# Four units' rows in flight and a later down product in a routed FFN's expert loop (one core, fp32 split in three)

## Chip, cores and metric

One core of one Trainium2 chip. The metric is the device time of one execution in microseconds, the median of the runs. The kernel before takes 964.21 us.

## What is computed

A linear attention with elu feature maps and a mixture of experts, both on the same input of 16 batches x 512 tokens x 256, summed with the input. The part around the change is the mixture: each of the 8192 tokens goes through 4 of 16 experts, each an up product, silu, and a down product weighted by the router.

```python
combine = zeros((T, E)).at[arange(T)[:, None], topk_idx].add(topk_w)   # T = 8192, E = 16, TOP_K = 4
up = jnp.einsum('th,ehi->eti', x, expert_up)                            # 256 -> 128
down = jnp.einsum('eti,eih->eth', jax.nn.silu(up), expert_down)         # 128 -> 256
moe_out = jnp.einsum('te,eth->th', combine, down)
shared = jax.nn.silu(x @ shared_up) @ shared_down
x = x + attention(layernorm(x)) + (moe_out + shared)
```

## The kernel before

All five engines run programs written out in full, with semaphores between them. Until about 490 us the 16 batches go through attention, shared FFN and router, and GpSimd scatters each token's row (its inputs, weights and running sum) into a region of its experts in HBM. A plan then splits the regions into 143 **units** of 256 rows of one expert: 128 that the tokens could fill, and 15 for the experts' remainders. From then on every engine goes through the units in order:

- **SP** loads a unit's rows (`load_rows`, 272 KB, its `dma_start` is line 453) and, later, its running sums (`load_sums`, line 465). Rows of unit u wait for `fu_done`, the count of up products: from unit 16 on for up(u-6). In each step the sums of the unit 3 before follow; they wait for `added`, the landings of the scatters of the 8th unit before and of those on which its tokens depend. Rows and sums have 8 buffers each.
- **PE** in step u: up product of u (helper `split3`, line 326; 6 matmuls, since each fp32 product is made from high and low parts: high by high, high by low, low by high), transposing of the rows of u+2 (`turn_rows`, line 1572, 4 transposes into a bank `A[u % 2]`), and the down product of u-1 (`unit_down`, 6 matmuls, into `A[2]`, `A[3]` or the two halves of `bank_y` in turn).
- **ACT** in step u: silu of u (line 800), the high part of the transposed rows of u+2 (`rows_high`, line 762), the high part of the silu values of u (line 805), a copy of the expert's up weights for u+2 (`stage`, line 774, into 4 buffers). The last 15 units' rows are loaded by ACT, under a condition.
- **VectorE** in step u: the rows' weights (line 1320) and the low part of the transposed rows of u+2 (`rows_low`, line 1323), the low part of the silu values of u (`hidden_rest`, line 1365), then for u-1 (`sum_up`) the ids of where each row goes on (line 1336, needs the sums loaded) and the weighted sum (line 1341, two instructions, needs the down product).
- **GpSimd** scatters the sums of u back to HBM, in two indirect DMAs (line 628). They wait for VectorE's sum, for the landing of the scatter of u-4, and from unit 10 on the first also for the down product of u+1, the second for the up product of u+3.

Semaphores: `fx_done`, `fx_hi`, `fx_lo` rows transposed, high, low; `fu_done` up product; `fs_done` silu; `fh_hi`, `fh_lo` silu values high, low; `fd_done` down product; `y_ready` summed. The trace names the tiles by their memory: rows `xn` or `x_in`, transposed rows high and low `xt_h`, `xt_l`, silu `hid`, its parts `hs_h`, `hs_l`, weights `k_h` or `k_l_p`, up product `bank_x`, down product `bank_a` or `bank_y` from `we`.

## Time and profile before

| | |
|---|---|
| median of 3 runs | 964.21 us (960.75 to 968.95) |
| profiled execution | 958.44 us, of it the span of the profile 956.7 us |
| experts' loop | about 490 to 925 us of the span, 143 units |
| busy share over the span | PE 80%, VectorE 74%, GpSimd 61%, ACT 58% |
| DMA | 194.66 MB, mean 203 GB/s over the span |
| granted TensorE clock, mean over the span | 0.945 of full |

The profile is one execution taken by the hardware profiler, times in us from the span's start. A line of the profile is a line of the kernel file. PE's matmuls are pipelined and their ends are modelled, so a busy PE isn't PE at its peak. The releaser of a wait is inferred from semaphore events; "issue" means that nothing the profile shows was waited for, "remote" that the releaser is not told.

### The profile page before, as it was taken

The page shows a single profiled execution, that of the slowest core. Times are in us where ns is not written, and L with a number is a line of the kernel's source. Part 1 is how long each engine was busy: PE and PEld are TensorE (multiplying, and loading weights), DVE is VectorE, ACT ScalarE, POOL GpSimd, SP SyncE. Part 2 cuts the span into 40 slices and gives each one's busy share as a digit, 9 for nine tenths or more (in the row PEclk, how much of TensorE's full clock was granted, in tenths as well). Part 3 has the DMA queues.
Part 4 walks back from the last instruction along what each step waited for, and adds up shares of the span by engine and source line. Part 5 has one row for each costly group of instructions (what it writes and reads, how often), then busy time and mean ns, then how long its engine had stood idle before and what let it go on. Part 6 is the DMA issues. An engine that isn't in the chain of part 4 may idle for free.

```text
span 956.7 us, 19946 instructions
## 1 busy us (share of the span) xinstructions
PE 762.2 (80%) x5232; PEld 696.8 (73%) x5232; DVE 703.3 (74%) x2409; ACT 559.5 (58%) x1174; POOL 579.6 (61%) x581
## 2 busy tenths in 40 slices
PE   4999999999999999997377776766777767767762
PEld 4899898999889988886266666765666767656751
DVE  6989988888888999988366766656666566666653
ACT  5778777777677766663155655445555455545541
POOL 1077766666777766667455556665666566565554
PEclk9999999999999999999699999899899799899897
DMA  5245545554445433333398888888788878889790
GB/s 157 89 161 191 187 176 187 190 187 180 145 160 193 147 124 125 119 114 124 121 330 256 267 259 263 259 260 257 240 265 256 256 241 267 263 247 283 232 341 19
DMA packets 137551, 194.66 MB, mean 203 GB/s; under 512 B 16593, under 2 KB 112993, under 8 KB 137441
## 3 DMA queue, kind: packets, MB, share of 16 engines
q1 hardware_dynamic: 107200, 109.23, 38.9%
q0 software_dynamic: 28064, 81.93, 22.2%
q10 hardware_dynamic: 2176, 2.23, 0.8%
q8 instruction: 45, 0.74, 0.4%
q14 instruction: 66, 0.53, 0.2%
HBM read 104.19 MB, written 105.04 MB: 219 GB/s over the span
## 4 chain that ended last, share of the span: by engine, by line
PE 62%; DVE 14%; issue 12%; another core or an unknown queue 5%; ACT 3%; DMA 2%; DVEq 1%; POOL 0%; SPq 0%; ACTq 0%; POOLq 0%
PE bank_a L326 27%; PE bank_x L326 14%; PE bank_y L326 14%; PE bank_a L1572 5%; DVE hs_l L1365 2%; DVE xn L1110 2%; DVE xn L1341 2%; DVE xt_l L1323 1%; PE bank_a L1412 1%; ACT xt_h L762 1%; DVE w L1320 1%; DMA xn<-in_L_attn_bo_dram 1%; DMA k_f<-rows_by_expert 1%; DVE k_f L1341 1%
## 5 line engine op out<-in xcount | busy, mean ns | idle before, releaser
L539 POOL DMA_INDIRECT rows_by_expert<-xn,slots_now x192 | 195.4, 1018 | 120.3 <-PE bank_a L326 63.0
L628 POOL DMA_INDIRECT rows_by_expert<-xn,f_id x128 | 125.5, 981 | 84.9 <-issue 28.1
L1323 DVE TENSOR_TENSOR xt_l<-bank_a,xt_h 128x512 fp32r<-128x512 f32 x143 | 98.2, 687 | 90.9 <-ACT xt_h L762 69.1
L326 PE MATMUL bank_a<-we,hs_h 128*128 x288 | 67.6, 328 | 94.3 <-DVE hs_l L1365 58.1
L800 ACT ACTIVATE hid<-bank_x 128x256 f32<-128x256 f32 x143 | 55.1, 385 | 142.6 <-PE bank_x L326 74.7
L762 ACT CAST xt_h<-bank_a 128x512 fp32r<-128x512 f32 x143 | 83.8, 586 | 80.7 <-PE bank_a L1572 47.5
L326 PEld LDWEIGHTS bank_a<-we,hs_h 128*128 128x128 f32 x288 | 49.0, 206 | 108.8 <-issue 108.8
L545 POOL DMA_INDIRECT rows_by_expert<-xn,slots_now x64 | 80.0, 1250 | 29.8 <-issue 13.2
L326 PE MATMUL bank_y<-we,hs_h 128*128 x284 | 68.6, 334 | 36.9 <-DVE hs_l L1365 20.5
L326 PE MATMUL bank_y<-ws,hs_h 128*128 128x256 f32 x512 | 95.4, 284 | 0.5 <-DVE hs_l L1078 0.5
L326 PE MATMUL bank_x<-xt_h,ws 128*128 128x512 f32 x256 | 92.1, 401 | 0.1
L326 PEld LDWEIGHTS bank_y<-we,hs_h 128*128 128x128 f32 x284 | 50.3, 210 | 50.4 <-issue 49.8
L326 PEld LDWEIGHTS bank_y<-ws,hs_h 128*128 128x128 f32 x512 | 81.8, 190 | 4.2 <-DVE hs_l L1078 0.7
L326 PE MATMUL bank_y<-ws,hs_l 128*128 128x256 f32 x256 | 72.7, 284 | 0.0
L326 PE MATMUL bank_x<-xt_h,k_h 128*128 128x256 f32 x288 | 70.2, 305 | 0.8 <-DVE xt_l L1323 0.8
L326 PE MATMUL bank_x<-xt_h,k_l_p 128*128 128x256 f32 x284 | 66.6, 296 | 1.4 <-DVE xt_l L1323 1.4
L710 ACT ACTIVATE k_f<-bank_a,minus_one 128x256 f32<-128x256 f32 x64 | 30.3, 474 | 57.7 <-issue 41.2
L1365 DVE TENSOR_TENSOR hs_l<-hid,hs_h 128x256 fp32r<-128x256 f32 x143 | 59.9, 419 | 3.5 <-issue 1.8
L805 ACT CAST hs_h<-hid 128x256 fp32r<-128x256 f32 x143 | 59.5, 416 | 0.1
L675 ACT ACTIVATE hid<-bank_x 128x512 f32<-128x512 f32 x64 | 37.7, 589 | 34.1 <-remote 24.4
L326 PEld LDWEIGHTS bank_x<-xt_h,k_h 128*128 128x128 f32 x288 | 55.8, 214 | 1.1 <-DVE xt_l L1323 1.0
L326 PEld LDWEIGHTS bank_x<-xt_h,ws 128*128 128x128 f32 x256 | 48.2, 188 | 9.2 <-DVE ws L922 0.3
(314 smaller groups left out, 2601.2 us busy)
## 6 DMA issues: line engine op xcount, KB each, us to landing
xn<-rows_by_expert SPq DMA_DIRECT2D x132, 272.0 KB
x_in<-rows_by_expert SPq DMA_DIRECT2D x80, 272.0 KB
rows_by_expert<-spare SPq DMA_DIRECT2D x22, 544.0 KB
x_in<-in_L_attn_x_dram SPq DMA_DIRECT2D x16, 512.0 KB
out_dram<-rows_by_expert SPq DMA_DIRECT2D x16, 512.0 KB
k_f<-rows_by_expert SPq DMA_DIRECT2D x16, 272.0 KB
q_f<-rows_by_expert SPq DMA_DIRECT2D x16, 272.0 KB
spare<-rows_by_expert SPq DMA_DIRECT2D x16, 272.0 KB
```

Source lines behind the costliest of these rows:

```text
L326: last = nc.tensor.matmul(dst, a, b, start=start and k == 0, stop=stop and k == n - 1, skip_group_check=mixed)
L539: G.indirect_dma_start(out=half_rows[:, :], in_=xn[:, c % NB, s, 0:RW], in_offset=None, out_offset=bass.IndirectOffsetOnAxis(ap=slots_now[ ...
L545: G.indirect_dma_start(out=by_expert[:, :], in_=xn[:, c % NB, s, :], in_offset=None, out_offset=bass.IndirectOffsetOnAxis(ap=slots_now[:, ...
L628: G.indirect_dma_start(out=half_rows[:, :], in_=f_y[u % YB][:, tile], in_offset=None, out_offset=offset).then_inc(added[u % CLS], 16)
L675: S_.activation(hid[:, n % 2], X[n % 2][:, :], ACT.Silu).then_inc(silu_done, 1)
L710: S_.activation(k_f[:, s, :], A[s][:, 0:D], ACT.Exp, bias=minus_one[:, 0:1])
L762: S_.copy(f_h[u % 4], A[u % 2][:, :].rearrange("p (c s t) -> p c s t", c=KD, s=2)).then_inc(fx_hi, 1)
L800: S_.activation(f_hid[u % 2], X[u % 2][:, 0:UR], ACT.Silu).then_inc(fs_done, 1)
L805: S_.copy(f_hh[u % 2], f_hid[u % 2]).then_inc(fh_hi, 1)
L1323: V.tensor_tensor(f_l[u % 4], A[u % 2][:, :].rearrange("p (c s t) -> p c s t", c=KD, s=2), f_h[u % 4].bitcast(F32), ALU.subtract).then_inc ...
L1365: V.tensor_tensor(f_hl[u % 2], f_hid[u % 2], f_hh[u % 2].bitcast(F32), ALU.subtract).then_inc(fh_lo, 1)
L1572: last = T_.transpose(A[u % 2][:, (2 * h + tile) * P:(2 * h + tile + 1) * P], f_rows[u % RB][:, tile, h * P:(h + 1) * P], ident[:, :])
```

## The change

From unit 14 (`FROM`) on, PE, ACT and VectorE treat the rows of u+3 in step u (transpose, high part, low part), and the down product and the weighted sum are those of u-2. In step 14 itself the rows of two units are treated (16 and 17) and there is no down product. For this the transposed rows rotate over four banks `A[0..3]`, the down product of a unit lies in one bank of `bank_y` (both tiles side by side, units in turn), the high and low parts of the silu values have 3 buffers, the rows' weights 8. The gates follow: GpSimd's second scatter of u waits for the up product of u+4 from unit 14 on; SP's rows of u wait for up(u-7) rather than up(u-6) from unit 16 on; the sums are loaded 5 steps behind the rows rather than 3 from there; ACT's loads of the last rows go out one step earlier. The copy of the up weights (`stage`) stays 2 ahead. The core of the diff:

```diff
@@ -265,14 +265,17 @@
         c_ends_i, c_ends_n = [reused(over_beats, (1, B), i * B, 1)[:, 0].bitcast(U32) for i in range(2)]
         c_before = reused(over_beats, (1, B), 2 * B, 1)[:, 0]
         c_class_i, c_class_n, c_need = [reused(over_beats, (CLS, B), (3 + i * CLS) * B, 1).bitcast(U32) for i in range(3)]
-        w2 = sb("w2", [P, 4, 2])
+        WB = 8
+        AB = 4
+        FROM = 14
+        w2 = reused(over_beats, (WB, 2), E * E - WB * 2)
         f_h = [reused(xt_h, (KD, 2, P), i * KD * UR) for i in range(4)]
         f_l = [reused(xt_l, (KD, 2, P), i * KD * UR) for i in range(4)]
         f_w = [reused(t, (2, UPW), i * 2 * UPW) for t in (k_h, k_l_p) for i in range(2)]
         f_hid = [reused(hid, (1, UR), i * UR)[:, 0] for i in range(2)]
-        f_hh = [reused(hs_h, (1, UR), i * UR)[:, 0] for i in range(2)]
-        f_hl = [reused(hs_l, (1, UR), i * UR)[:, 0] for i in range(2)]
-        f_dn = [[A[2], A[3]], [Y[:, 0, :], Y[:, 1, :]]]
+        f_hh = [reused(hs_h, (1, UR), i * UR)[:, 0] for i in range(3)]
+        f_hl = [reused(hs_l, (1, UR), i * UR)[:, 0] for i in range(3)]
+        f_dn = [[Y[:, i, t * D:(t + 1) * D] for t in range(2)] for i in range(2)]
 
         wk_loaded, wq_loaded, wo_loaded, wv_loaded, bias_loaded = sems(
             "wk_loaded", "wq_loaded", "wo_loaded", "wv_loaded", "bias_loaded")
@@ -364,6 +367,17 @@
             else:
                 eng.wait_ge(raw_loaded, 64 * (i - SH + 3 if i else 1))
 
+        def turned_with(u):
+            if u in (0, FROM):
+                return {0: (), FROM: (u + 2, u + 3)}[u]
+            v = u + (2 if u < FROM else 3)
+            return (v,) if 1 < u and v < UNITS else ()
+
+        def down_with(u):
+            if u < 3 or u == FROM:
+                return ()
+            return (u - 1 if u < FROM else u - 2,)
+
         def unit_rows(first_row, half):
             return by_expert[bass.ds(first_row, UR), half * RW:(half + 1) * RW].rearrange("(s p) r -> p s r", p=P)
 
@@ -440,7 +454,7 @@
             row_of = {}
 
             def load_rows(u):
-                wait(sp, fu_done, u - RB + (3 if u >= 2 * RB else 1))
+                wait(sp, fu_done, u - RB + (2 if u >= 2 * RB else 1))
                 if u == 4:
                     sp.wait_ge(attn_ready, SUB * B)
                 row = row_of[u] = four_from(mybir.EngineType.SP, 0, u, 0, SLOTS - UR)
@@ -468,7 +482,7 @@
 
             ROWS_AHEAD = 7
             SUMS_AHEAD = 4
-            for u in range(SUMS_BY_ACT + ROWS_AHEAD - SUMS_AHEAD):
+            for u in range(SUMS_BY_ACT + ROWS_AHEAD - SUMS_AHEAD + 2):
                 if LAST_SET_LOADED <= u < LAST_SET_LOADED + SET_PARTS:
                     load_set_part(SH + E - 1, u - LAST_SET_LOADED)
                 if u == EARLY - 1:
@@ -479,6 +493,8 @@
                 elif u < SUMS_BY_ACT:
                     row_of[u] = four_from(mybir.EngineType.SP, 0, u, 0, SLOTS - UR)
                 v = u - (ROWS_AHEAD - SUMS_AHEAD)
+                if u >= 2 * RB:
+                    v = u - 5 if u >= 2 * RB + 2 else -1
                 if 0 <= v < EARLY // 2 or EARLY - 1 <= v < SUMS_BY_ACT:
                     load_sums(v)
 
@@ -622,7 +638,7 @@
                         if tile == 0:
                             pool.wait_ge(fd_done, min(u + 2, UNITS))
                         else:
-                            pool.wait_ge(fu_done, min(u + 4, UNITS))
+                            pool.wait_ge(fu_done, min(u + (4 if u < FROM else 5), UNITS))
                     offset = bass.IndirectOffsetOnAxis(ap=f_id[:, u % YB, tile:tile + 1], axis=0)
                     if u < SKIPPED:
                         G.indirect_dma_start(out=half_rows[:, :], in_=f_y[u % YB][:, tile], in_offset=None,
@@ -759,7 +775,7 @@
             def rows_high(u):
                 act.wait_ge(fx_done, u + 1)
                 wait(act, fu_done, u - 3)
-                S_.copy(f_h[u % 4], A[u % 2][:, :].rearrange("p (c s t) -> p c s t", c=KD, s=2)).then_inc(fx_hi, 1)
+                S_.copy(f_h[u % 4], A[u % AB][:, :].rearrange("p (c s t) -> p c s t", c=KD, s=2)).then_inc(fx_hi, 1)
 
             act.wait_ge(plan_ready, 1)
 
@@ -798,11 +814,11 @@
                 act.wait_ge(fu_done, u + 1)
                 wait(act, fh_lo, u - 1)
                 S_.activation(f_hid[u % 2], X[u % 2][:, 0:UR], ACT.Silu).then_inc(fs_done, 1)
-                if 1 < u and u + 2 < UNITS:
-                    rows_high(u + 2)
+                for v in turned_with(u):
+                    rows_high(v)
                 act.wait_ge(fs_done, u + 1)
-                wait(act, fd_done, u - 1)
-                S_.copy(f_hh[u % 2], f_hid[u % 2]).then_inc(fh_hi, 1)
+                wait(act, fd_done, u - 2)
+                S_.copy(f_hh[u % 3], f_hid[u % 2]).then_inc(fh_hi, 1)
                 if u == 1:
                     rows_high(2)
                     stage(2)
@@ -812,8 +828,8 @@
                     stage(u + 2)
                 if u in (4, 18):
                     set_high(SH + E - 2 + (u == 18))
-                if SKIPPED <= u + 6 < UNITS:
-                    load_last_rows(u + 6)
+                if SKIPPED <= u + 7 < UNITS:
+                    load_last_rows(u + 7)
                 if u >= SUMS_BY_ACT:
                     load_last_sums(u)
 
@@ -1316,11 +1332,11 @@
             def rows_low(u):
                 expert = expert_from(experts, u)
                 dve.wait_ge(rows_loaded[u % RB], 16 * (u // RB + 1))
-                wait(dve, y_ready, u - 3)
-                V.tensor_copy(w2[:, u % 4, :], f_rows[u % RB][:, :, bass.ds(expert + D, 1)]
+                wait(dve, y_ready, u - WB + 1)
+                V.tensor_copy(w2[:, u % WB, :], f_rows[u % RB][:, :, bass.ds(expert + D, 1)]
                               .rearrange("p s o -> p (s o)")).then_inc(w2_ready, 1)
                 dve.wait_ge(fx_hi, u + 1)
-                V.tensor_tensor(f_l[u % 4], A[u % 2][:, :].rearrange("p (c s t) -> p c s t", c=KD, s=2),
+                V.tensor_tensor(f_l[u % 4], A[u % AB][:, :].rearrange("p (c s t) -> p c s t", c=KD, s=2),
                                 f_h[u % 4].bitcast(F32), ALU.subtract).then_inc(fx_lo, 1)
 
             def sum_up(u):
@@ -1338,7 +1354,7 @@
                 dve.wait_ge(w2_ready, u + 1)
                 for tile in range(2):
                     y = f_y[u % YB][:, tile, 0:D]
-                    last = V.scalar_tensor_tensor(out=y, in0=f_dn[u % 2][tile][:, 0:D], scalar=w2[:, u % 4, tile:tile + 1],
+                    last = V.scalar_tensor_tensor(out=y, in0=f_dn[u % 2][tile], scalar=w2[:, u % WB, tile:tile + 1],
                                                   in1=y, op0=ALU.mult, op1=ALU.add)
                 last.then_inc(y_ready, 1)
 
@@ -1362,12 +1378,12 @@
 
             def hidden_rest(u):
                 dve.wait_ge(fh_hi, u + 1)
-                V.tensor_tensor(f_hl[u % 2], f_hid[u % 2], f_hh[u % 2].bitcast(F32), ALU.subtract
+                V.tensor_tensor(f_hl[u % 3], f_hid[u % 2], f_hh[u % 3].bitcast(F32), ALU.subtract
                                 ).then_inc(fh_lo, 1)
 
             rows_low(0)
             rows_low(1)
-            for u in range(UNITS + 1):
+            for u in range(UNITS + 2):
                 if u == 2:
                     sum_up(1)
                     hidden_rest(2)
@@ -1375,8 +1391,8 @@
                     hidden_rest(3)
                     sum_up(2)
                 next_experts(experts, mybir.EngineType.DVE, u)
-                if 1 < u and u + 2 < UNITS:
-                    rows_low(u + 2)
+                for v in turned_with(u):
+                    rows_low(v)
                 if u < UNITS and u not in (2, 3):
                     hidden_rest(u)
                 if u == 1:
@@ -1384,7 +1400,8 @@
                     rows_low(2)
                     rows_low(3)
                 if u >= 4:
-                    sum_up(u - 1)
+                    for v in down_with(u):
+                        sum_up(v)
                 if u in (3, 16):
                     set_shape(SH + E - 2 + (u == 16))
                 if u in (6, 20):
@@ -1566,10 +1583,10 @@
 
             def turn_rows(u):
                 pe.wait_ge(rows_loaded[u % RB], 16 * (u // RB + 1))
-                wait(pe, fx_lo, u - 1)
+                wait(pe, fx_lo, u - AB + 1)
                 for h in range(KD):
                     for tile in range(2):
-                        last = T_.transpose(A[u % 2][:, (2 * h + tile) * P:(2 * h + tile + 1) * P],
+                        last = T_.transpose(A[u % AB][:, (2 * h + tile) * P:(2 * h + tile + 1) * P],
                                             f_rows[u % RB][:, tile, h * P:(h + 1) * P], ident[:, :])
                 last.then_inc(fx_done, 1)
 
@@ -1583,15 +1600,15 @@
                 moving = [we[:, bass.ds(expert, 1), i, UPW:].rearrange("p o d -> p (o d)") for i in range(2)]
                 pe.wait_ge(fh_lo, v + 1)
                 wait(pe, y_ready, v - 1)
-                if v == 1:
+                if v == 0:
                     pe.wait_ge(y_summed, B)
                 for tile in range(2):
                     cols = slice(tile * P, (tile + 1) * P)
-                    last = split3(f_dn[v % 2][tile][:, 0:D],
-                                  [(f_hh[v % 2][:, cols], f_hl[v % 2][:, cols], moving[0], moving[1])])
+                    last = split3(f_dn[v % 2][tile],
+                                  [(f_hh[v % 3][:, cols], f_hl[v % 3][:, cols], moving[0], moving[1])])
                 last.then_inc(fd_done, 1)
 
-            for u in range(UNITS + 1):
+            for u in range(UNITS + 2):
                 next_experts(experts, mybir.EngineType.PE, u)
                 if u < UNITS:
                     pe.wait_ge(fx_lo, u + 1)
@@ -1601,15 +1618,15 @@
                            [(f_w[u % 4][:, 0, h * I:(h + 1) * I], f_w[u % 4][:, 1, h * I:(h + 1) * I],
                              f_h[u % 4][:, h].rearrange("p s t -> p (s t)"),
                              f_l[u % 4][:, h].rearrange("p s t -> p (s t)")) for h in range(KD)]).then_inc(fu_done, 1)
-                if 1 < u and u + 2 < UNITS:
-                    turn_rows(u + 2)
+                for v in turned_with(u):
+                    turn_rows(v)
                 if u == 1:
                     unit_down(0)
                     turn_rows(2)
                     unit_down(1)
                     turn_rows(3)
-                if u >= 3:
-                    unit_down(u - 1)
+                for v in down_with(u):
+                    unit_down(v)
 
 
 # ---- launch: one core; inputs and outputs as the reference has them ----
```

## Rows read from the trace of the kernel before

**Rows 1.** Stretches: us, busy us (instructions), clock, DMA share; DMA of 560 to 900.

```profile
core 0: us, PE busy (x) PEld busy (x) DVE busy (x) ACT busy (x) POOL busy (x), PEclk, DMA share, GB/s
490.00:500.00 10.00, 6.72 (x45) 6.28 (x45) 5.61 (x17) 5.10 (x12) 4.72 (x5) 0.83 1.00 331
560.00:600.00 40.00, 30.58 (x213) 27.85 (x213) 26.87 (x88) 22.22 (x52) 24.50 (x26) 0.93 0.85 267
600.00:650.00 50.00, 35.11 (x242) 32.32 (x241) 29.83 (x89) 25.41 (x60) 30.02 (x31) 0.91 0.85 259
650.00:700.00 50.00, 33.55 (x235) 30.41 (x234) 29.69 (x89) 25.44 (x60) 28.94 (x31) 0.93 0.83 249
700.00:750.00 50.00, 37.47 (x264) 34.17 (x263) 32.15 (x97) 25.88 (x62) 30.91 (x33) 0.93 0.81 252
...
925.00:957.00 32.00, 10.10 (x75) 8.79 (x73) 13.44 (x41) 7.95 (x19) 16.13 (x17) 0.79 0.30 89
...
DMA packets 66442, 87.41 MB, mean 257 GB/s; under 512 B 6668, under 2 KB 59690, under 8 KB 66396
```

**Rows 2.** Groups, 560 to 900 us: busy us, mean ns | idle before, releasers.

```profile
L628 POOL DMA_INDIRECT rows_by_expert<-xn,f_id x104 | 101.7, 978 | 68.5 <-issue 23.5 <-PE bank_y L326 14.5 <-remote 8.8
L1323 DVE TENSOR_TENSOR xt_l<-bank_a,xt_h 128x512 fp32r<-128x512 f32 x104 | 71.5, 687 | 72.4 <-ACT xt_h L762 54.5 <-issue 17.8
...
L1365 DVE TENSOR_TENSOR hs_l<-hid,hs_h 128x256 fp32r<-128x256 f32 x104 | 43.5, 418 | 0.0
...
L1572 PE MATMUL bank_a<-ident,xn 128*128 128x128 f32 x208 | 34.4, 292 | 0.0
...
L774 ACT CAST k_h<-we 128x512 fp32r x52 | 32.7, 629 | 0.0
...
L1336 DVE TENSOR_TENSOR f_id<-xn,nowhere 128x2 uint32<-128x2 uint32 x51 | 8.0, 157 | 0.0
```

**Rows 3.** Who waited for whom, 560 to 900 us: total, times, longest.

```profile
ACT hid L800 <- PE bank_x L326: 57.4, 38, 4.6
DVE xt_l L1323 <- ACT xt_h L762: 54.5, 22, 4.0
...
PE bank_a L326 <- DVE hs_l L1365: 46.7, 20, 4.2
ACT xt_h L762 <- PE bank_a L1572: 28.6, 20, 3.9
...
ACT xt_h L762 <- remote: 25.2, 12, 3.9
```

**Rows 4.** Timeline of smooth units: start, us, instruction, [idle before].

```profile
704.96 0.17 DVE L1320 COPY w<-xn 128x2 f32 x1 [0.29 <-DVE k_f L1341]
...
707.11 0.41 ACT L805 CAST hs_h<-hid 128x256 fp32r<-128x256 f32 x1
...
707.28 0.17 DVE L1320 COPY w<-xn 128x2 f32 x1 [0.37 <-issue]
...
707.41 0.62 ACT L774 CAST k_h<-we 128x512 fp32r x1
...
707.96 0.42 DVE L1365 TENSOR_TENSOR hs_l<-hid,hs_h 128x256 fp32r<-128x256 f32 x1
...
708.72 0.51 PE L326 MATMUL bank_y<-we,hs_h 128*128 x2 [0.19 <-issue]
...
709.53 0.28 PE L326 MATMUL bank_x<-xt_h,k_h 128*128 128x256 f32 x1
```

**Rows 5.** Timeline around one hole.

```profile
716.28 0.96 POOL L628 DMA_INDIRECT rows_by_expert<-x_in,f_id  x1 [0.30 <-issue]
...
716.83 0.60 PE L1572 MATMUL bank_a<-ident,x_in 128*128 128x128 f32 x4
717.55 0.96 POOL L628 DMA_INDIRECT rows_by_expert<-x_in,f_id  x1 [0.30 <-issue]
...
719.62 0.58 ACT L762 CAST xt_h<-bank_a 128x512 fp32r<-128x512 f32 x1 [3.91 <-remote]
...
720.24 0.69 DVE L1323 TENSOR_TENSOR xt_l<-bank_a,xt_h 128x512 fp32r<-128x512 f32 x1 [3.91 <-ACT xt_h L762]
```

## The prediction

> **What bounds the kernel now.** I read the stretches first, to see what the experts' loop costs a unit, then the groups of instructions of 560 to 900 us, then who waited for whom, and last the timeline of one smooth unit and of one hole.
>
> The loop starts near 490 us and ends near 925. In 560 to 900 us line 1323 runs 104 times [rows 2], so a unit takes 340 / 104 = 3.27 us. No engine is full: VectorE is busy 0.59 to 0.67 of a stretch, the DMA engines 0.81 to 0.85 [rows 1]. VectorE's own work of a unit is seen where nothing is late: from one start of line 1320 to the next, 704.96 to 707.28, it takes 2.32 us [rows 4]. GpSimd's is two scatters of 0.98 us [rows 2] and the 0.30 us between two of them [rows 5], 2.56 us. The transfers need 87.41 MB / 104 = 840 KB a unit [rows 1]; at the 331 GB/s of the stretch with a share of 1.00 that is 2.54 us, and by the share 3.27 x 0.83 = 2.71 us. So about 0.56 us of each unit (3.27 - 2.71) is nobody's work.
>
> Who is late? Not the loads: PE's transposes (line 1572) and VectorE's line 1336, which are the first to need rows and sums, have 0.0 us of idle time before them [rows 2]. VectorE waits 54.5 us in 22 waits for ACT's line 762, ACT in turn 57.4 us for the up product and 28.6 and 25.2 us at line 762 for the transposes, PE 46.7 us for line 1365 [rows 3]. The hole of 715 to 720 us shows how they fit [rows 5]. PE has transposed the rows that ACT's line 762 is due to split, and another unit's at 716.83, yet line 762 starts at 719.62 after 3.91 us, and VectorE 3.91 us late behind it. GpSimd had just issued scatters at 716.28 and 717.55, and the wait ends 1.1 us after the second. So PE's signal, not its work, is late, and it comes after a run of scatters. I can't show from this the cause of the delay, only the coincidence. The Trainium skill (Perfetto Trace Analysis, Per-engine timelines) says that TensorE's end in a profile is an estimate and that its semaphore moves only after PSUM's acknowledgement; this agrees with a recorded end of 717.4 us and a release at 719.6, but puts no price on it.
>
> **The change, part by part.** Nothing is computed more or less: 143 units, the same matmuls, copies and transfers. The bank of the down product, the 8 pairs of weights and the third silu buffer change addresses alone, cost 0.
>
> *Transposing 3 ahead, down product 2 behind.* In before, PE's order is up(u), rows(u+2), down(u-1); up(u+1) stands behind down(u-1), and down(u-1) waits for line 1365 of unit u-1. In the smooth unit line 1365 ends at 708.38, down starts at 708.72 and the next up product at 709.53 [rows 4]. After, down(u-2) stands there, whose silu values are a unit old. The up product then waits only for the weights of line 774, which are still copied 2 ahead, and which ended at 708.03 [rows 4]: 1.50 us earlier. If ACT is a unit ahead of VectorE, the gain of lead is a whole unit, 2.32 us. Each wait of VectorE for ACT lasts 54.5 / 22 = 2.48 us, the longest 4.0 [rows 3]. Hiding 1.50 us of each of the 22 gives 33 us, 2.32 us of each at most 51 us, in 104 units: 0.32 to 0.49 us a unit. The other side is 0: a signal that is late by more than the lead is still late, and a lead that is used up must be won back in the 0.95 us between 2.32 and 3.27.
>
> *GpSimd's gate.* The scatters of u wait for down(u+1) and for up(u+3), after for up(u+4). Queued behind them on GpSimd are only the next scatters; those who wait for them are SP's loads of sums and the scatter of u+4. In before, the unit's sum comes right after line 1365 of u+1, and down(u+1) and up(u+3) are issued after that same instruction, so the gate is always just about binding and paces the scatters. After, the sum comes a unit later and PE has posted both before. The pacing is weaker. Its bound is one pair more in a run of scatters, 2.56 us of delay more for PE's signal: it could eat the lead of 1.50 to 2.32 us entirely.
>
> *SP's queue.* Rows are issued when up(u-7) rather than up(u-6) is done, transposed one unit earlier: the four units between stay. Sums are issued one unit later and used one unit later: the same. The two steps more of SP's, VectorE's and PE's loops issue nothing new. ACT's conditional loads of the last 15 units go out one unit earlier. All is covered by the loads' 0.0 us of idle [rows 2]; with the cover gone a late landing would stop PE's whole queue.
>
> *The switch at unit 14.* Two sets of rows are transposed, split and subtracted in one step (one more pass of 0.69 us on VectorE [rows 2]) and no down product is made: about +1 us, once.
>
> *The sum.* The step acts on units 14 to 127, 113 of them; the later ones are partly empty and the tail of 925 to 957 us has a DMA share of 0.30 [rows 1] and isn't touched. Between 0 and 0.49 us a unit I go by the nearest row of the kernel itself: how fast it runs where its holes are few. PE's 16 matmuls and transposes a unit (6, 4, 6) give units from the counts: 264 in 700 to 750 us are 16.5 units, 3.03 us each; 213 in 560 to 600 are 13.3, 3.00 us; 235 in 650 to 700 are 14.7, 3.40 us [rows 1]. I take 3.03 us as what the deeper order keeps up: 3.27 - 3.03 = 0.24 us, x 113 = 27 us, +1 for the switch, so -26 us. Against the profiled execution's own 958.4 us (its span is 956.7) this gives 932; the runs' median, 964.2, lies 0.6% higher, and with it the forecast is 938 us.
>
> **The rivals.**
>
> *A, the transfers bound.* All signals are hidden, and the loop runs at the pace of the DMA engines: 3.27 - 2.71 = 0.56 us, x 113 = 63 us, so 902 us. For: the share of 0.81 to 0.85 over the whole loop, and loads that are never late. Against: more than the 51 us per 104 units that the lead can hide, and GpSimd's 2.56 us is as near. The Trainium skill (HBM Reference, Specifications (TRN2)) gives about 358 GB/s effective per core; by it the unit's transfers would need 2.35 us, and an estimate of the loop's floor would be lower still; the trace's own stretch with a share of 1.00 moved 331 GB/s.
>
> *B, the late signal moves along.* The scatters, less paced, close up, and what the lead hides the longer runs take back. 2.56 us of one more pair against 1.50 to 2.32 us of lead is an even trade, 3.27 us stays: 955 to 974 us, most likely 964. For: in [rows 5] the wait ends with the run of scatters, as if bound to it. Against: a run ends also when sums run out, and those come at VectorE's 2.32 us or slower, GpSimd's pairs at 2.56.
>
> *C, slower.* The same mechanism from the point where a run grows by two pairs: 2 x 2.56 = 5.1 us more, less 2.32 of lead, is 2.8 us for each such hole. If one in three of the 22 waits grows so, that is 7 x 2.8 = 20 us in 104 units, 21 us in 113, and PE, idle longer, runs more of the time at the lower of its two levels (granted 0.91 to 0.93 of full now [rows 1]): 985 us.
>
> *D, it does nothing.* PE can't use the lead since line 774's copy, still 2 ahead, holds the up product. It would show 0 as B does and is counted with it. The 1.50 us of [rows 4] speak against it.
>
> **How the numbers follow.** The forecast, -10 to -38 us (926 to 954), gets 0.45; A and what lies between it and the forecast (under 926) 0.12; B with D (955 to 974) 0.27; C 0.16. About 1% is what a measurement of this kernel can tell from no change. So faster by over 1%: 0.45 + 0.12 = 0.57; within: 0.27; slower: 0.16. For the range I leave out about a tenth at each end: 914 (part of A) to 976 (most of C). The likeliest case's own range is 926 to 954.
>
> **What would show it.** Right: VectorE's waits at line 1323 for ACT fall from 54.5 us per 340 to under 30; 104 units take 315 us rather than 340; DMA share near 0.90; PE's idle time before the down product for line 1365 almost gone, since it is a unit old. A: share above 0.95, and idle time before line 1572 or 1336. B: ACT's waits at 762 and 800 as long as now, with GpSimd's idle time before line 628 smaller and runs of more than four scatters. C: the same with PEclk below 0.85. The forecast is wrong if the holes are as many as now and only longer or shorter by what GpSimd does, or if the sums' loads, one unit later, begin to be late.

## The result, and the profile after

| | before | after |
|---|---|---|
| median of 6 runs each | 964.22 us (960.75 to 968.95) | 955.1 us (953.05 to 956.38) |
| ratio, 95% interval | | 0.9895 (0.987 to 0.992) |
| profiled execution | 958.44 us, span 956.7 us | 955.79 us, span 954.0 us |
| granted TensorE clock, mean over the span | 0.945 | 0.930 |

The change takes 9.1 us, 1.05%. The forecast was 26 us: it has the sign right and the size three times too large. The time lies inside the range, but in the band of case B (955 to 974 us). The two profiled executions are only 2.6 us apart, because that of before lies 6 us under its median; in these two traces the units 14 to 142 take 415.0 and 411.5 us, so the rows below show 3.5 us of the gain and not all nine.

The stretch of 560 to 900 us of after, the groups of the same stretch (busy us, mean ns of one, idle time before it and what ended it), and who waited for whom (total, times, longest):

```profile
core 0: us, PE busy (x) PEld busy (x) DVE busy (x) ACT busy (x) POOL busy (x), PEclk, DMA share, GB/s
560.00:900.00 340.00, 247.24 (x1674) 228.39 (x1672) 208.12 (x634) 175.13 (x414) 202.30 (x210) 0.88 0.83 258
```

```profile
L644 POOL DMA_INDIRECT rows_by_expert<-xn,f_id x104 | 100.2, 963 | 70.5 <-issue 25.2 <-PE bank_y L329 19.8 <-remote 14.3
L1339 DVE TENSOR_TENSOR xt_l<-bank_a,xt_h 128x512 fp32r<-128x512 f32 x104 | 71.6, 689 | 93.6 <-ACT xt_h L778 80.8 <-issue 12.5
L329 PE MATMUL bank_y<-we,hs_h 128*128 x420 | 100.8, 333 | 6.5 <-DVE xn L1357 3.6 <-DVE x_in L1357 1.0 <-DVE spare L1357 0.6
L329 PE MATMUL bank_x<-xt_h,k_l_p 128*128 128x256 f32 x208 | 52.3, 312 | 23.2 <-DVE xt_l L1339 11.9 <-ACT k_l_p L790 9.6 <-issue 1.7
L329 PE MATMUL bank_x<-xt_h,k_h 128*128 128x256 f32 x208 | 52.3, 312 | 16.7 <-issue 11.1 <-DVE xt_l L1339 5.6
L1589 PE MATMUL bank_a<-ident,x_in 128*128 128x128 f32 x212 | 39.7, 318 | 26.9 <-DMA x_in<-rows_by_expert 13.9 <-issue 12.9
L1589 PE MATMUL bank_a<-ident,xn 128*128 128x128 f32 x208 | 34.9, 294 | 17.5 <-DMA xn<-rows_by_expert 12.6 <-issue 4.8
```

```profile
DVE xt_l L1339 <- ACT xt_h L778: 80.8, 30, 5.2
ACT hid L816 <- PE bank_x L329: 56.4, 35, 4.5
ACT hid L816 <- remote: 39.4, 16, 4.6
ACT xt_h L778 <- remote: 26.5, 8, 4.7
ACT xt_h L778 <- PE bank_a L1589: 23.5, 18, 3.9
```

What to see in them:

- 104 units in 340 us again, and the DMA share is 0.83, as in [rows 1, 2]. The sum gave 315 us for 104 units and a share near 0.90.
- What the change removes is removed. In before the down product waited 71.8 us in one group and 23.6 us in the other, 46.7 and 12.2 us of it for line 1365 (the two groups stand below); all its high-part matmuls now have 6.5 us of idle time before them.
- The waits did not go, they moved. The up product now waits 39.9 us (23.2 + 16.7, before 0.0), the transposes 44.4 us (26.9 + 17.5, before 0.0), and 26.5 us of that for rows that hadn't landed.
- VectorE's waits for ACT's high part are 80.8 us in 30, the longest 5.2; they were 54.5 in 22, the longest 4.0 [rows 3]. The forecast had them under 30 us.
- GpSimd's waits for PE's posts did not shrink either: 40.2 us in 27 waits for the down product in before, 39.3 in 24 in after.

The groups of before that the second point goes by, then GpSimd's waits for the down product, first of before and then of after, all of 560 to 900 us:

```profile
L326 PE MATMUL bank_a<-we,hs_h 128*128 x208 | 49.0, 329 | 71.8 <-DVE hs_l L1365 46.7 <-issue 25.0
L326 PE MATMUL bank_y<-we,hs_h 128*128 x212 | 52.2, 339 | 23.6 <-DVE hs_l L1365 12.2 <-issue 11.4
```

```profile
POOL rows_by_expert L628 <- PE bank_y L326: 25.4, 18, 1.7
POOL rows_by_expert L628 <- PE bank_a L326: 14.8, 9, 1.7
```

```profile
POOL rows_by_expert L644 <- PE bank_y L329: 39.3, 24, 2.5
```

The timeline of a hole in after (start, us, instruction, [idle before]) beside which [rows 5] stand:

```profile
729.85 0.96 POOL L644 DMA_INDIRECT rows_by_expert<-xn,f_id  x1 [1.75 <-PE bank_y L329]
731.11 0.96 POOL L644 DMA_INDIRECT rows_by_expert<-xn,f_id  x1 [0.30 <-issue]
...
731.84 0.60 PE L1589 MATMUL bank_a<-ident,x_in 128*128 128x128 f32 x4
...
732.38 0.96 POOL L644 DMA_INDIRECT rows_by_expert<-k_f,f_id  x1 [0.31 <-issue]
...
733.64 0.96 POOL L644 DMA_INDIRECT rows_by_expert<-k_f,f_id  x1 [0.30 <-issue]
...
733.93 0.60 PE L1589 MATMUL bank_a<-ident,x_in 128*128 128x128 f32 x4
...
734.91 0.96 POOL L644 DMA_INDIRECT rows_by_expert<-q_f,f_id  x1 [0.30 <-issue]
...
736.18 0.96 POOL L644 DMA_INDIRECT rows_by_expert<-q_f,f_id  x1 [0.31 <-issue]
...
738.46 0.59 ACT L778 CAST xt_h<-bank_a 128x512 fp32r<-128x512 f32 x1 [2.52 <-remote]
...
739.07 0.69 DVE L1339 TENSOR_TENSOR xt_l<-bank_a,xt_h 128x512 fp32r<-128x512 f32 x1 [5.20 <-ACT xt_h L778]
...
739.24 0.62 ACT L790 CAST k_l_p<-we 128x512 fp32r x1
...
739.96 0.55 PE L329 MATMUL bank_x<-xt_h,k_l_p 128*128 128x256 f32 x1 [4.67 <-ACT k_l_p L790]
```

Three pairs of scatters, 0.30 us apart. PE's transposes of 731.84 and 733.93 are recorded as over at 732.44 and 734.53; ACT's line 778, which waits here for nothing but PE, starts at 738.46, 1.3 us after the sixth scatter ends. It is the picture of [rows 5] with a longer run.

The trace also keeps the times of semaphore updates (not of all: four in five of PE's, a third or so of the transfers'), and those show the lateness itself. In this hole none of PE's is recorded from 735.52 us on until five come from 738.43 to 738.72, the first 0.03 us before line 778 starts; in the hole of [rows 5] there is none from 715.31 to 719.60, then four in 0.21 us. The landings of transfers bunch in the same way: 14 updates are recorded from 731.00 to 738.25 and 47 from 738.25 to 739.50, though the transfers' packets go on ending through the hole (149 a microsecond from 735.50 to 738.25, 168 in the 4.5 us before). So it isn't PE alone that is late: the posts of transfers are too.

The last two lines show a second thing. PE's next up product starts 0.1 us after ACT's copy of the up weights (line 790), the one that is still made 2 units ahead, and that copy stands behind line 778 in ACT's program. It is so throughout 560 to 900 us: PE is silent (no matmul and no weight load recorded) for more than 0.5 us 17 times before an up product, 38.1 us together, and each of the 17 ends 0.07 us after the end of a copy of line 790, while the low part of the same unit's rows had been ready for 3.7 to 7.4 us.

Runs of scatters, counted from the timeline over 560 to 900 us, with a run as scatters less than 0.45 us apart: in before a run has 2.9 scatters on average (35 of 72 runs are a single pair), in after 4.0 (4 is the commonest). That is 1.1 scatters more a run, at 1.27 us each 1.4 us, against a lead that was put at 1.50 to 2.32 us. GpSimd's idle time in the stretch is the same (136.6 us before, 137.7 after), in fewer and longer pieces. ACT's own waits of over 1.5 us fell in number from 50 to 37 but their sum only from 120.4 to 114.4 us: fewer holes, each longer.

### The profile page after: what moved, and what is told of

Its sections match the earlier page's. It is cut to its first block, busy times and chain, and to the rows that moved or that the text cites. A ratio compares the mean times of both kernels' runs of the same rounds, so it can differ in the third digit from the quotient of the medians.

```text
span 954.0 us, 19939 instructions
## 1 busy us (share of the span) xinstructions
PE 767.1 (80%) x5232; PEld 704.9 (74%) x5232; DVE 698.2 (73%) x2409; ACT 558.9 (59%) x1174; POOL 578.0 (61%) x581
## 4 chain that ended last, share of the span: by engine, by line
PE 57%; issue 12%; DVE 9%; DMA 7%; another core or an unknown queue 5%; SPq 4%; POOL 2%; ACT 2%; POOLq 1%; DVEq 0%; ACTq 0%
PE bank_a L329 21%; PE bank_y L329 16%; PE bank_x L329 14%; PE bank_a L1589 4%; DMA rows_by_expert<-xn,f_id 2%; DMA x_in<-rows_by_expert 2%; DVE xn L1126 2%; POOL rows_by_expert L644 2%; PE bank_a L1429 1%; DMA xn<-rows_by_expert 1%; DVE xt_l L1339 1%; SPq L467 1%; SPq L339 1%; ACT xt_h L778 1%
## 5 line engine op out<-in xcount | busy, mean ns | idle before, releaser
L644 POOL DMA_INDIRECT rows_by_expert<-xn,f_id x128 | 123.3, 963 | 89.9 <-issue 30.8
L329 PE MATMUL bank_y<-we,hs_h 128*128 x572 | 136.4, 331 | 23.1 <-issue 7.2
L329 PEld LDWEIGHTS bank_y<-we,hs_h 128*128 128x128 f32 x572 | 100.1, 210 | 32.4 <-issue 31.0
L329 PE MATMUL bank_x<-xt_h,k_l_p 128*128 128x256 f32 x284 | 70.9, 310 | 33.0 <-DVE xt_l L1339 16.5
L329 PE MATMUL bank_x<-xt_h,k_h 128*128 128x256 f32 x288 | 72.4, 312 | 27.0 <-issue 14.4
L329 PE MATMUL bank_y<-we,hs_l 128*128 x286 | 85.8, 300 | 0.0
L329 PEld LDWEIGHTS bank_x<-xt_h,k_l_p 128*128 128x128 f32 x284 | 55.0, 213 | 35.7 <-DVE xt_l L1339 28.0
L1589 PE MATMUL bank_a<-ident,x_in 128*128 128x128 f32 x284 | 51.3, 310 | 28.7 <-DMA x_in<-rows_by_expert 15.7
L1357 DVE SCALAR_TENSOR_TENSOR xn<-bank_y,over_beats,xn 128x256 f32<-128x256 f32 x144 | 62.7, 477 | 15.1 <-remote 8.9
L1589 PEld LDWEIGHTS bank_a<-ident,x_in 128*128 128x128 f32 x284 | 36.7, 158 | 35.2 <-DMA x_in<-rows_by_expert 21.1
```

Source lines behind the costliest of these rows:

```text
L329: last = nc.tensor.matmul(dst, a, b, start=start and k == 0, stop=stop and k == n - 1, skip_group_check=mixed)
L644: G.indirect_dma_start(out=half_rows[:, :], in_=f_y[u % YB][:, tile], in_offset=None, out_offset=offset).then_inc(added[u % CLS], 16)
L1357: last = V.scalar_tensor_tensor(out=y, in0=f_dn[u % 2][tile], scalar=w2[:, u % WB, tile:tile + 1], in1=y, op0=ALU.mult, op1=ALU.add)
L1589: last = T_.transpose(A[u % AB][:, (2 * h + tile) * P:(2 * h + tile + 1) * P], f_rows[u % RB][:, tile, h * P:(h + 1) * P], ident[:, :])
```

## The experiments

What was open after this comparison: do late signals after runs of scatters keep the pace (and does GpSimd's gate hold them short), or is it the rows that now land late, or the bytes; and which part of the change brings the nine microseconds. The "time of a unit" below is the mean over units 20 to 120 of a profile, from one first weighted sum (line 1341, 1357 in after) to the next: 3.257 us in before, 3.237 in after.

Each set of runs had the kernel before beside it. In the third and the last set it took 837 us instead of 962, and what set off the difference is not known (the last section has what the records show of it); those two sets are read by their ratios alone, and not against the others. The experiments needed SyncE's waits on loaded numbers written a little differently from the two kernels, first with a mask, then with 16-bit loads; both forms turned out to be experiments themselves.

### The mask alone, on both kernels

```diff
-sp.wait_ge(added[k], four_from(mybir.EngineType.SP, 2 + k, u, PRIMED, PRIMED + 32 * UNITS))
+sp.wait_ge(added[k], four_from(mybir.EngineType.SP, 2 + k, u, PRIMED, PRIMED + 32 * UNITS) & 8191)
```

> The kernel before with every wait against a loaded number going through a bitwise and with 8191 on its way (four more register operations a unit on SyncE, the numbers are the same). It is the control of all experiments. Both theories expect 964 us within 1% (955 to 974): SyncE's queue is waited for by nobody in the kernel before, whose transposes have 0.0 us of idle time before them.

> The changed kernel with the same bitwise and. Both theories expect 955 us within 1%. If the extra register operations cost something here and not in the kernel before, up to +10 us, SyncE's queue has become part of the path with the change, since its transposes now wait 44 us for rows in 560 to 900 us.

Measured: 980.22 us and 977.72 us, beside 963.1 (ratios 1.018, 1.0092 to 1.0267, and 1.0185, 1.0097 to 1.0274). Both missed their expected times, by 16 and 23 us. In the loop the edit is four register operations a unit on SyncE (the same mask stands before ACT's loads of the last 15 units' sums, and before SyncE's loads at both ends of the loop). The intervals of the two overlap: whether the change still gains under the mask can't be told. The groups of the masked kernel before, 560 to 900 us, show what they do:

```profile
L1572 PE MATMUL bank_a<-ident,x_in 128*128 128x128 f32 x200 | 35.5, 305 | 36.6 <-DMA x_in<-rows_by_expert 33.8 <-issue 2.6
L1572 PE MATMUL bank_a<-ident,xn 128*128 128x128 f32 x200 | 33.8, 294 | 37.2 <-DMA xn<-rows_by_expert 29.9 <-issue 7.2
```

From 0.0 [rows 2] to 73.8 us of idle time. SyncE's queue had little room: the 0.0 us said that rows came in time, not that there was room. In after, SyncE's own waits for others fall from some 39 to some 13 us in the 340, and the rows are late even without the mask. The change adds no instruction to a unit's part of that queue. What grew is the number of its instructions that take about 0.7 us instead of under 0.4: 101 in before, 135 in after, an estimated 20 us more from these counts, which is most of the room that is gone.

### A quarter of the rows' bytes

Only the first 68 of 272 columns of each row are loaded, so the outputs are not the reference's. On top of the mask, so the masked kernels are the controls.

```diff
-sp.dma_start(f_rows[u % RB], unit_rows(row, 0))
+sp.dma_start(f_rows[u % RB][:, :, 0:RW // 4], unit_rows(row, 0)[:, :, 0:RW // 4])
```

> The control before, with only the first 68 of 272 columns of each unit's rows loaded (the rest of the buffer keeps old contents, so the mixture's result is not the reference's; numbers of instructions, packets and waits are the same). It takes 204 KB of a unit's 840 KB away. Theory S (PE's signals, held back while scatters are in flight, set the pace): the loop keeps its 3.26 us a unit, 955 to 970 us. Theory T (the transfers set the pace, at a share of 0.83): a quarter of the bytes less gives 0.4 to 0.8 us a unit, 113 to 128 units, 45 to 100 us less: 865 to 920 us.

> The changed kernel with only the first 68 of 272 columns of each unit's rows loaded (the mixture's result is not the reference's). Theory S: 945 to 960 us, only the 44 us of waits for rows in 560 to 900 us may shrink, and ACT's waits for PE stay. Theory T: as in the kernel before or more, 850 to 905 us, and the changed kernel then wins by more than 1% over the other, because its lead can be used.

Measured: 979.46 and 979.55 us (1.0199, 1.0112 to 1.0285, and 1.0189, 1.0104 to 1.0274), the same as their controls. The stretch of 560 to 900 us of the kernel after with small rows:

```profile
560.00:900.00 340.00, 233.16 (x1609) 214.32 (x1609) 204.40 (x613) 172.69 (x401) 192.03 (x200) 0.90 0.67 189
```

The DMA share is down to 0.67 and 189 GB/s, and no time is won. The transposes still wait 69.7 us for rows (79.8 in the control): what is late there is the issue of the loads, not their bytes. Because the masked kernels are held by SyncE's queue, this pair alone doesn't say that bytes are free in the unmasked kernel; f6 below does that with rows in time.

### 16-bit loads alone, on both kernels

```diff
-table[i:i + 1, u // P, first % P:first % P + 4]
+table.bitcast(mybir.dt.uint16)[i:i + 1, u // P, 2 * (first % P):2 * (first % P) + 8:2]
```

> The kernel before with the numbers to be waited against loaded as the low 16 bits of the table's words, with no operation added anywhere: a control whose queues are as long as in the kernel before. Theory Q (SyncE's queue is so full that an operation more on it costs its whole time; the bitwise ands cost 17 us) expects 955 to 970 us, the time of the kernel before. If it is as slow as with the bitwise ands (975 to 985 us), it wasn't their number but what the numbers pass through, and Q falls.

> The changed kernel with the same 16 bit loads, a control. Theory Q: 950 to 960 us, and faster than the other control by 5 to 13 us, as the changed kernel was over the kernel before. Otherwise as for the other control.

Measured beside 963.71 us: 976.77 (1.0127, 1.0041 to 1.0213) and 969.75 (1.0083, 1.0054 to 1.0111). Missed too, and in the same way: in the traces the mean of SyncE's register loads is 0.82 and 0.84 us rather than 0.28 and 0.30 (one in five of them still loads 32-bit numbers), some 0.67 us more in a unit's queue. That costs 13 us on the kernel before and about as much on the kernel after (969.75 against the 955.1 of the result, 15 us). By the medians after is 7 us faster than before in this form as well, but the intervals of the two overlap.

### SyncE's queue emptied: rows loaded from ACT's queue

```diff
-                if u < SKIPPED:
+                if u < 24:
                     load_rows(u)
...
-                if SKIPPED <= u + 7 < UNITS:
+                if 24 <= u + 7 < UNITS:
                     load_last_rows(u + 7)
```

(`u + 6` in the kernel before; 16-bit loads in both.)

> The 16 bit control of the kernel before, with the rows of units 24 to 127 loaded from ACT's queue, in its step 6 units ahead, rather than from SyncE's; SyncE keeps its wait for the up product, and the sums. Theory Q: the kernel before waited little for SyncE (0.0 us before its transposes), so there is little to win, and ACT's queue gets 0.4 to 1 us a unit more: 955 to 975 us. Theory S (only PE's held signals count): the same, 955 to 975 us.

> The 16 bit control of the changed kernel, with the rows of units 24 to 127 loaded from ACT's queue, 7 units ahead. Here the theories part. Theory Q (the lead is there, but rows come late since SyncE's queue is full): with the queue lighter the rows are in time, the transposes' waits of 44 us in 560 to 900 us fall under 10 us, and the loop gains 0.15 to 0.3 us a unit, 15 to 30 us: 920 to 942 us. Theory S (PE's held signals, released after runs of scatters, set the pace in both): the waits for rows vanish but ACT's waits for PE grow by as much: 950 to 965 us.

Measured beside 963.71 us: 970.47 (1.0065, 1.0027 to 1.0102) and 958.61 (0.9944, 0.991 to 0.9978). Rows are in time in both. The groups of e4, 560 to 900 us:

```profile
L1349 DVE TENSOR_TENSOR xt_l<-bank_a,xt_h 128x512 fp32r<-128x512 f32 x106 | 73.0, 689 | 103.1 <-ACT xt_h L783 90.3 <-issue 12.5
L1599 PE MATMUL bank_a<-ident,x_in 128*128 128x128 f32 x216 | 39.5, 315 | 0.0
L1599 PE MATMUL bank_a<-ident,xn 128*128 128x128 f32 x208 | 35.5, 299 | 0.0
```

This is the main test of "late rows ate the gain", and the answer is mostly no. The transposes wait for nothing now, 11 us are won against the 16-bit kernel after, and yet the unit takes 3.238 us, as in after. VectorE's waits for ACT grew to 90.3 us. The 920 to 942 us of the theory that late rows alone had cost the gain were not reached. The test isn't quite clean, since ACT's queue has the issues of the loads instead (0.38 us each).

Where PE stands still shows what took the late rows' place: its silences of more than 0.5 us, 560 to 900 us, counted from the traces. f4 is e4 once more, and f7 is its form with the down product 1 unit behind, as in before; both stand further down.

| | before | after | e4 | f4 | f7 |
|---|---|---|---|---|---|
| all, us (number) | 85.6 (42) | 82.9 (52) | 84.3 (33) | 81.9 (34) | 95.0 (41) |
| before the down product | 85.6 (42) | 5.1 (4) | 12.5 (10) | 11.6 (11) | 95.0 (41) |
| before the transposes | 0 | 39.6 (31) | 0 | 0 | 0 |
| before the up product, ended by the copy of line 790 (795 in e4 and f4) | 0 | 38.1 (17) | 71.8 (23) | 70.3 (23) | 0 |

With the rows in time PE goes on further and stops at the up product, for the up weights, which ACT still copies 2 units ahead. The sum of its silences hardly changes. One such hole of f4, where the profile doesn't name the releaser:

```profile
740.46 0.58 ACT L783 CAST xt_h<-bank_a 128x512 fp32r<-128x512 f32 x1 [4.62 <-remote]
...
741.25 0.62 ACT L795 CAST k_l_p<-we 128x512 fp32r x1
...
741.97 0.55 PE L329 MATMUL bank_x<-xt_h,k_l_p 128*128 128x256 f32 x1 [4.63 <-issue]
```

No run copied the weights 3 ahead, so what this stop costs has no price of its own.

### Bytes, gates and the two halves of the change, first set

Four edits beside each other: GpSimd's two gates taken away; the scatters and sums thinned to 16 of their columns (so outputs are not the reference's); rows 3 ahead alone; down product 2 behind alone. All on the kernel after with rows from ACT's queue.

> The changed kernel with 16 bit loads and rows loaded from ACT's queue (rows in time), and without GpSimd's waits for the down product of u+1 and the up product of u+4 from unit 10 on: the scatters start as soon as the sums are made. Theory P (the pacing by the gates keeps the scatters apart, and without it runs grow and PE's signals are held longer): slower than 958.6 us by 5 to 25 us. Theory R (the gates bind only because PE's signals are late, and pace nothing): within 1% of 958.6 us, or up to 10 us faster.

> The changed kernel with 16 bit loads and rows from ACT's queue, whose scatters and loads of the sums carry only the 16 pointer columns of 272 (the sums are not carried from expert to expert, and the output is copied from the input, so the result is not the reference's). The same number of indirect DMAs with the same 128 rows each, 9.4 times fewer bytes a row; VectorE has one small operation a unit more. Theory B (PE's signals are held until the scatters' writes of 139 KB have landed): the holds shrink, ACT's waits for PE fall by more than half, 3.24 us a unit become 2.6 to 2.9: 890 to 930 us. Theory G (they are held by GpSimd's making of the descriptors, 0.98 us each): the holds stay, 945 to 965 us.

> One part alone, beside e4_after_rows_act (958.6 us) and e3_before_rows_act (970.5 us): rows transposed 3 units ahead over four banks from unit 14 on, the down product 1 unit behind as before; 16 bit loads and rows from ACT's queue as in those two. If the gain of 12 us between those two comes from the transposes' lead: 955 to 963 us. If from the later down product: 966 to 975 us, since the up product again stands behind a down product that waits for line 1365.

> The other part alone: down product 2 units behind from unit 14 on, rows transposed 2 ahead; 16 bit loads and rows from ACT's queue. If the later down product gives the gain: 955 to 963 us. If it needs both (with rows 2 ahead ACT has no transposed rows to split while PE's signals are late): 966 to 975 us.

Measured: 846.27 (1.012, 1.0085 to 1.0156), 841.66 (1.0055, 1.0032 to 1.0078), 853.81 (1.0234, 1.0184 to 1.0283) and 844.55 us (1.0121, 1.0071 to 1.0172). But the kernel before took 836.74 us beside them. The rows of e5, 500 to 780 us, show that this is another regime:

```profile
500.00:780.00 280.00, 237.48 (x1784) 227.69 (x1784) 216.79 (x677) 198.60 (x448) 210.58 (x216) 0.93 0.97 330
```

```profile
L1344 DVE TENSOR_TENSOR xt_l<-bank_a,xt_h 128x512 fp32r<-128x512 f32 x112 | 76.7, 685 | 11.4 <-ACT xt_h L778 11.4
```

VectorE waits 11.4 us for ACT in 280 us with no gate at all, the DMA share is 0.97, and the scatters follow each other every 1.28 us on average without a single break of 0.45 us, a pair in 2.57 us. That is the floor of GpSimd from [rows 2, 5], reached. PE's signals are not late there, so the set can't say what makes them late; it was repeated with the same edits.

### The same edits, second set

Beside these the kernel before took 961.85 us (959.28 to 965.32).

f4 is e4 again, the control:

> The same kernel as e4 (changed kernel, 16 bit loads, rows from ACT's queue), as the base of the three others beside it. If the kernel before takes about 964 us here: 955 to 963 us. If it takes about 837 us, whose loop is bound by GpSimd's two scatters (2.56 us a unit): 0.5 to 2% slower than the kernel before, as e5 and e8 were.

Measured 959.61 us (0.9979, 0.9958 to 1.0).

f5 takes the gates away:

```diff
-                        if tile == 0:
-                            pool.wait_ge(fd_done, min(u + 2, UNITS))
-                        else:
-                            pool.wait_ge(fu_done, min(u + (4 if u < FROM else 5), UNITS))
```

> The same kernel as e5: f4 without GpSimd's waits for the down and the up product. Beside a kernel before of 964 us: theory P (the gates pace the scatters, and keep PE's signals from being held longer) 5 to 25 us slower than f4; theory R (the gates pace nothing) within 8 us of f4. Beside one of 837 us: within 4 us of f4, as nothing holds the signals there.

Measured 1001.49 us (1.0404, 1.0381 to 1.0428), 42 us over f4. The direction was that of the theory that the gates keep the runs short and the signals in time; the size was far beyond what it had expected. A group of f5, 560 to 900 us, and its timeline around a hole:

```profile
L1344 DVE TENSOR_TENSOR xt_l<-bank_a,xt_h 128x512 fp32r<-128x512 f32 x95 | 65.4, 688 | 154.9 <-ACT xt_h L778 105.4 <-issue 49.4
```

```profile
706.75 0.96 POOL L644 DMA_INDIRECT rows_by_expert<-spare,f_id  x1 [2.55 <-DVE spare L1362]
...
713.07 0.96 POOL L644 DMA_INDIRECT rows_by_expert<-xn,f_id  x1 [0.30 <-issue]
715.31 0.59 ACT L778 CAST xt_h<-bank_a 128x512 fp32r<-128x512 f32 x1 [3.91 <-remote]
715.93 0.69 DVE L1344 TENSOR_TENSOR xt_l<-bank_a,xt_h 128x512 fp32r<-128x512 f32 x1 [5.60 <-ACT xt_h L778]
```

95 units in the 340 us instead of 106. Now 28 of 34 runs have six scatters (mean 5.6), and the wait ends 1.3 us after the last of them again. So with this kernel and these signals a scatter that comes when it can, rather than when PE has posted, costs 42 us. PE's posts show the same picture as in the hole of after: none from 710.99 to 715.29, then five in 0.30 us.

f6 is the thin one. The scatters and the loads of the sums carry 16 of 272 columns, with as many scatters of as many rows as before. Their numbers are worked out for the narrower rows (100 or so short VectorE instructions more in the stretch).

```diff
-G.indirect_dma_start(out=by_expert[:, :], in_=f_y[u % YB][:, tile], ...
+G.indirect_dma_start(out=thin_rows, in_=f_y[u % YB][:, tile, D:RW], ...
```

> The same kernel as e6: f4 with scatters and loads of the sums of 16 columns rather than 272 (the result is not the reference's: sums aren't carried, the output is a copy of the input). Beside a kernel before of 964 us: theory B (PE's signals and SyncE's instructions are late behind bytes on their way) 2.6 to 2.9 us a unit rather than 3.24, 30 to 75 us less than f4; theory G (behind GpSimd's making of descriptors) within 10 us of f4. Beside one of 837 us: 0 to 8 us less than f4.

Measured 957.26 us (0.9958, 0.9944 to 0.9972), 2.4 us under f4, which is not clear of the noise (the intervals overlap). The stretch of f6 and its waits, then the same waits of f4, 560 to 900 us:

```profile
560.00:900.00 340.00, 257.13 (x1695) 243.79 (x1696) 226.79 (x757) 179.07 (x428) 205.72 (x212) 0.85 0.41 96
```

```profile
DVE xt_l L1351 <- ACT xt_h L785: 75.0, 23, 4.8
```

```profile
DVE xt_l L1349 <- ACT xt_h L783: 79.4, 23, 5.2
```

A DMA share of 0.41 at 96 GB/s, and 23 waits as in f4. So the late signals don't depend on the bytes that are moved. The scatters are as many, as long (967 ns) and in runs as long (4.4, f4 4.0). Of the causes that were put to a test, the making of the scatters on GpSimd, or their number, is left; that the scatters are the cause at all rests on where the holes end and on f5. The Trainium skill (DMA: Bandwidth & Descriptors, SWDGE vs HWDGE vs iDMA) says that software on a core of GpSimd computes the descriptors of a transfer that is issued there; a scatter of 272 columns takes 964 ns in f4 and one of 16 columns 967 ns in f6, which agrees with work that doesn't go by the bytes. No run here says why PE's posts should wait for that.

f7 does the first half of the change alone: rows 3 ahead, the down product 1 behind as before (with it the gate `u + 4` and the sums' loads one unit earlier, since both belong to the down product's place).

```diff
-            return (u - 1 if u < FROM else u - 2,)
+            return (u - 1,) if 3 <= u <= UNITS else ()
```

> The same kernel as e7: rows transposed 3 ahead, down product 1 unit behind, 16 bit loads and rows from ACT's queue. Beside a kernel before of 964 us: near f4 (within 5 us) if the transposes' lead brings the gain of 12 us of e4 over e3, 6 to 15 us slower than f4 if the later down product does. Beside one of 837 us: 0.5 to 1.5% slower than f4, as it was against e8.

Measured 969.08 us (1.0075, 1.0046 to 1.0105), 9.5 us slower than f4 and level with e3 by ratio (1.0065). Its down product, 560 to 900 us:

```profile
L329 PE MATMUL bank_y<-we,hs_h 128*128 x416 | 101.4, 337 | 102.2 <-DVE hs_l L1389 60.7 <-issue 41.1
```

The wait of before, 71.8 + 23.6 us, is back at 102.2 (f4: 13.0). Transposing earlier brings nothing by itself; the gain of the change needs the down product's later place (with the gate and the sums' loads that f7 sets back with it; no run here tells these three apart). Whether it needs the rows' lead as well was only tried beside the kernel of 837 us (e8), where e8 is 9 us faster than e7. It stays open for the other condition.

### Gates drawn tighter

If a weaker gate eats the lead, a gate one unit tighter should give it back. g1 does that from unit 14 on, g2 sets the up product's gate alone back to `u + 4`; a smaller number is a looser gate, so g1 is the tightest, the kernel after lies between them, and g2 the loosest.

```diff
-                            pool.wait_ge(fd_done, min(u + 2, UNITS))
+                            pool.wait_ge(fd_done, min(u + (2 if u < FROM else 3), UNITS))
                         else:
-                            pool.wait_ge(fu_done, min(u + (4 if u < FROM else 5), UNITS))
+                            pool.wait_ge(fu_done, min(u + (4 if u < FROM else 6), UNITS))
```

> The kernel f4 (changed kernel, 16 bit loads, rows from ACT's queue) with GpSimd's gates one unit later from unit 14 on: the first scatter of u waits for the down product of u+2, the second for the up product of u+5. So they stand to the sum as they did in the kernel before. If the gain that was forecast went into the weaker pacing: faster than f4 by 8 to 25 us beside a kernel before of 962 us. If the gates of f4 pace as well as these: within 5 us of it; if they stop GpSimd for longer than the signals need, slower by up to 15 us. Beside a kernel before of 837 us: 0 to 15 us slower than there, since GpSimd's 2.56 us a unit is the bound and the gates only add to it.

> The kernel f4 with the second scatter's gate as in the kernel before, the up product of u+4-1 = u+3, one unit looser than f4's. From no gates at all (42 us slower) to f4 this is the step between: 2 to 15 us slower than f4 beside a kernel before of 962 us, if the second gate is what paces; within 3 us if it is the first. Beside one of 837 us: within 4 us of f4.

Measured: 860.37 us (1.0285, 1.0243 to 1.0326) and 849.06 (1.0153, 1.0122 to 1.0184), beside a kernel before of 837.29 us. So this pair fell into the condition in which signals aren't late, and there the tighter gates cost 11 us against the looser one. That fits with GpSimd as the bound. f4 itself wasn't run beside them, so the times expected against f4 stay unanswered. For the condition of the result the question is not answered. No kernel was run that is shown to beat the changed one at 955.1 us.

## Why the prediction was right or wrong

**Right: what was late, and the order of PE.** PE's signal, not its work, keeps the pace: every kernel of the 960 us condition has its VectorE waiting 48 to 105 us in 340 for ACT, and ACT for PE, and in the holes looked at PE's semaphore updates come together at the end. The up product did stand behind line 1365. With the down product a unit later that wait went from 95 to 6.5 us, and with the down product put back to 1 unit behind (f7 against f4, both with rows from ACT's queue) 9.5 us of time came back, about as much as the change had won.

**Right: not the transfers.** Case A had 0.12. Thin transfers (share 0.41, rows in time) change next to nothing.

**Wrong: the price of the lead.** The sum took off 0.24 us a unit (3.27 to 3.03); measured are 0.02 us in the two profiles (3.257 to 3.237) and, from the medians, 9.1 us over the 114 units from 14 to 127, 0.08 us each. The step that failed is "hiding 1.50 us of each of the 22" waits. The 1.50 us were read in a smooth unit [rows 4], where line 774's copy of the up weights is over long before PE comes to the up product. In a hole it isn't: the copy stands in ACT's program behind the silu and the high part that wait for PE's late posts. All 17 silences of PE before an up product in after, and all 23 in f4 with rows in time, end 0.07 us after such a copy, the rows' low part having been ready for over 3.6 us. This is case D, the copy still 2 ahead, which the prediction named and set aside with these same 1.50 us. PE's silences of over 0.5 us sum to 85.6 us in before and 82.9 in after: they went from the down product to the up product and the transposes. That the copy is where PE stops is shown; what a copy 3 ahead would give was not tried.

**Wrong: 3.03 us as a pace that can be kept up.** It was that of the fastest of the 40 to 50 us pieces of before, got by dividing PE's instructions by 16, and taken as the pace with fewer holes. It wasn't a piece with few holes: 700 to 750 us has 7 waits of ACT of over 1.5 us, its neighbours 7 and 8, and [rows 5] is one of the seven. A piece of 50 us holds 15 units, give or take one, by the count of line 1323 (14 to 16), so a fast piece says little. (From 14 to 127 there are 114 units, not 113; this changes nothing.)

**Wrong: GpSimd's runs at 0.** The prediction bounded the term at one pair more, 2.56 us, said that this "could eat the lead entirely", and left it out of the sum. Runs did grow by 1.1 scatters, VectorE's waits from 54.5 to 80.8 us, the longest from 4.0 to 5.2, and the time lies in the band of cases B and D. Of B's own signs one came (ACT's waits stay), one came in part (17 of 53 runs are of more than four scatters, against 9 of 72) and one didn't (GpSimd's idle time isn't smaller, and it waits as long for PE's posts). The argument against B, that sums come no faster than VectorE's 2.32 us, left out the sums that pile up while GpSimd waits. So the growth of the runs is shown, and f5 shows that gates matter, 42 us in all; that the looser gate made the runs grow is argued. PE's posts come in bursts, and a burst opens the gates of several scatters at once; this too would make runs, and no run here tells the two apart. How much of the missing 17 us belongs to the copy, to the longer runs and to late rows isn't separated.

**Wrong: SyncE's queue at 0.** "All is covered by the loads' 0.0 us of idle." Idle time of the consumer was read as slack of the producer. The mask shows that 4 register operations a unit cost 17 us already before the change, and in after the transposes wait 44.4 us. Of the sum's error this is the smaller part: with rows in time (e4, f4) the loop still took 3.21 to 3.24 us a unit, PE then standing at the up product.

**Open: the clock.** The granted clock fell from 0.91 to 0.88 of full in the stretch, with PE waiting differently; the transposes' mean rose from 286 to 318 ns in one group and stayed in the other. f4 had 0.83 and was no slower a unit (3.210 us), so it isn't the main thing, but no run separates its share.

## What to carry to other kernels

A lead is as long as its shortest part. When an engine is to run 3 units ahead, list everything that it waits for, and look at how far ahead each is made and behind what it stands in its maker's program; and take that from a unit in which something was late, not from a smooth one. An idle time of 0.0 before a consumer says that its loads come in time, not that the queue that feeds it has room; to know the room, add a few cheap instructions to the queue and look. Where a gate waits for another engine's posts, moving that engine's work deeper into a pipeline loosens the gate without touching it: work out again when it opens, and what then runs in a row. And before a wait is counted as hideable, ask what ends it: a wait that ends with another engine's burst grows with the burst.
